# Idle bf16 products on TensorE in the drain and the first attention rounds of a decoder layer

## What is computed

```
x = LN(x + state_space(x))          # 16 states per feature, scan over the 64 tokens of a sequence,
                                    # layer norm inside, projection W_out
x = LN(x + gated_attention(x, ctx)) # 4 heads of 32, causal, weights q.k * exp(cumulated log gates - row max),
                                    # divided by max(|row sum|, exp(-row max)), norm per head
x = LN(x + moe(x))                  # router of 8 experts, top 2, silu(x w1) * (x w3) w2, hidden size 512
```

## Time and profile before

| | us |
|---|---|
| median of 3 runs | 702.19 (701.72, 702.19, 706.64) |
| profiled execution | 706.54 |
| its span, first to last instruction | 704.9 |
| TensorE busy | 544.6 (77%) |
| VectorE busy | 430.6 (61%) |
| GpSimd busy | 369.7 (52%) |
| ScalarE busy | 329.5 (47%) |
| mean granted TensorE clock | 0.863 |

### The profile page before, as it was taken

One profiled execution on the slowest core, in us unless ns is written; L12 is line 12 of the kernel. 1 busy time (PEld: TensorE's weight loads), 2 busy tenths in 40 slices (PEclk: granted clock), 3 DMA queues, 4 the chain that ended last, 5 costly groups with the idle time before them and its releaser, 6 DMA issues.

```text
span 704.9 us, 10813 instructions
## 1 busy us (share of the span) xinstructions
PE 544.6 (77%) x3387; PEld 386.7 (55%) x3387; DVE 430.6 (61%) x880; ACT 329.5 (47%) x732; POOL 369.7 (52%) x301
## 2 busy tenths in 40 slices
PE   2589999899889888686384889797878689989800
PEld 0234434445344447675263768686667568988800
DVE  1599999999999941676748376656352612211155
ACT  2475685876867553122132435444443323333327
POOL 1497979999789752216506163625253533322341
PEclk9999999999999995555555789998898899999955
DMA  4434535444454532732341735361616157788594
GB/s 148 148 101 148 175 122 166 146 170 167 137 179 146 191 74 52 133 62 62 77 113 42 193 120 158 136 232 36 203 63 216 59 177 243 241 292 270 170 244 117
DMA packets 83319, 104.51 MB, mean 148 GB/s; under 512 B 40784, under 2 KB 64592, under 8 KB 83136
## 3 DMA queue, kind: packets, MB, share of 16 engines
q1 hardware_dynamic: 74576, 90.99, 42.4%
q0 software_dynamic: 4320, 8.92, 3.7%
q10 hardware_dynamic: 4368, 3.93, 2.0%
HBM read 91.48 MB, written 12.34 MB: 147 GB/s over the span
## 4 chain that ended last, share of the span: by engine, by line
PE 25%; issue 24%; POOL 20%; DVE 10%; DMA 9%; ACT 3%; SPq 2%; another core or an unknown queue 1%; POOLq 0%; ACTq 0%; DVEq 0%
POOL hc L640 12%; PE pB L1063 7%; PE pq L1076 4%; DMA wslot<-in_expert_w 4%; PE py L818 4%; PE py L1063 2%; POOL y_dram L745 2%; PE pC L997 1%; ACT x_all L1457 1%; DMA y_dram<-dx,xin 1%; PE pa L979 1%; POOL xg_dram L736 1%; DMA x_all<-y_dram 1%; POOL bcs L604 1%
## 5 line engine op out<-in xcount | busy, mean ns | idle before, releaser
L640 POOL TENSOR_TENSOR hc<-h,Crep 128x1024 f32<-128x1024 f32 x64 | 149.7, 2356 | 14.6 <-DVE h L1507 13.2
L745 POOL DMA_INDIRECT y_dram<-dx,xin x71 | 68.9, 971 | 153.9 <-ACT dx L1378 144.8
L1063 PE MATMUL pB<-Crep,wslot 128*128 128x256 f32 (+1 forms) x556 | 118.9, 360 | 21.9 <-DMA wslot<-in_expert_w 10.7
L818 PE MATMUL py<-hc,ident 128*128 128x512 f32 x256 | 120.7, 598 | 8.1 <-POOL hc L640 8.1
L1063 PEld LDWEIGHTS pB<-Crep,wslot 128*128 128x128 f32 x556 | 90.8, 204 | 38.7 <-DMA wslot<-in_expert_w 14.0
L1498 DVE TENSOR_TENSOR u<-dx,pC 128x1024 f32<-128x1024 f32 x64 | 77.3, 1207 | 17.4 <-PE pC L807 17.3
L818 PEld LDWEIGHTS py<-hc,ident 128*128 128x128 f32 x256 | 46.8, 189 | 53.9 <-issue 37.4
L1789 DVE TENSOR_TENSOR Crep<-u,pB 128x512 f32<-128x512 f32 x35 | 24.0, 686 | 85.5 <-PE pB L1063 42.2
L1507 DVE TENSOR_TENSOR_SCAN h<-pB,u 128x1024 f32<-128x1024 f32 x32 | 73.1, 2285 | 1.0 <-ACT pB L1196 0.6
L1507 DVE TENSOR_TENSOR_SCAN h<-pa,u 128x1024 f32<-128x1024 f32 x32 | 73.1, 2284 | 0.0
L1789 DVE TENSOR_TENSOR u<-u,pB 128x512 f32<-128x512 f32 x36 | 24.8, 688 | 78.9 <-PE pB L1063 46.0
(11 more groups left out here) (225 smaller groups left out, 952.0 us busy)
## 6 DMA issues: line engine op xcount, KB each, us to landing
wslot<-in_expert_w SPq DMA_DIRECT2D x46, 768.0 KB
Crep<-c_dram SPq DMA_DIRECT2D x64, 512.0 KB, 3.8
h<-m_dram SPq DMA_DIRECT2D x16, 256.0 KB
xin<-xg_dram SPq DMA_DIRECT2D x25, 130.0 KB
cT_st<-in_ctx_T SPq DMA_DIRECT2D x8, 256.0 KB, 4.1
dx<-in_ctx_T SPq DMA_DIRECT2D x8, 256.0 KB, 4.0
delta<-in_ctx_tok SPq DMA_DIRECT2D x32, 64.0 KB
hc<-y_dram SPq DMA_DIRECT2D x8, 256.0 KB, 8.5
```

The source lines that it names most:

```text
L640: nc.gpsimd.tensor_tensor(hc[:, K % 4], h[:, K % 3], Crep[:, K % 4].rearrange("p a t -> p (a t)"), ALU.mult).then_inc(hc_done, 1)
L745: nc.gpsimd.indirect_dma_start(out=y2_dram, out_offset=bass.IndirectOffsetOnAxis(ap=xin[:, i % NX, a, D:D + 1].bitcast(i32), axis=0), in_= ...
L818: last = nc.tensor.matmul(py[:], ident[:], hc[:, K % 4, i * CH:(i + 1) * CH], start=False, stop=(K % STEPS == STEPS - 1 and i == 1))
L1063: last = nc.tensor.matmul(bank[:, o * a * P:(o + 1) * a * P], wslot[:, i % NW, stage * F + f * P:stage * F + (f + 1) * P], xgT[i % 2][:, 0 ...
```

## The change

A helper `fill(n)` issues `n` products of `sel[:, 0]` with `bcs[:, 0]` (96 rows, 128 by 512, bf16) into `py`. It waits for nothing and signals nobody; its result is overwritten unread. It is called at 9 places of the drain, at up to 8 places of the rounds 0 to 3, and in front of `turn_m(1)`. Nothing on the other engines is touched.

```
+            def fill(n):
+
+                for _ in range(n):
+                    nc.tensor.matmul(py[:], sel[:, 0], bcs[:, 0], start=True, stop=True)
+
             sum_state(STEPS * NCH - 2)
             sum_state(STEPS * NCH - 1)
             turn_m(0)
             center_y(NCH - 1)
+            fill(4)
             scores(0, 0)
             variance(NCH - 1)
+            fill(3)
             turn_x1(NCH - 2)
+            fill(3)
             scores(0, 1)
+            fill(3)
             project(NCH - 1)
+            fill(4)
             gate_products(NCH - 2)
+            fill(4)
             scores(0, 2)
+            fill(3)
             weighted_values(0, 0)
+            fill(3)
             scores(0, 3)
+            fill(3)
             weighted_values(0, 1)
...
+                if c <= 3:
+                    fill(4)
                 if back:
                     turn_x2(c - 1)
                 expert_units(first[0:1])
+                if c <= 3:
+                    fill(6)
                 if front:
                     scores(c + 1, 1)
+                if c <= 3:
+                    fill(4)
                 if back:
                     logits(c - 1)
                 expert_units(first[1:3])
+                if c <= 3:
+                    fill(8)
                 if front:
                     scores(c + 1, 2)
                 expert_units(first[3:])
+                if c <= 2:
+                    fill(6)
                 if front:
                     scores(c + 1, 3)
                     weighted_values(c + 1, 0)
+                if c <= 2:
+                    fill(4)
...
                 if front:
                     weighted_values(c + 1, 1)
                 expert_units(second[1:3])
+                if c <= 2:
+                    fill(8)
                 if back:
                     ranks(c - 1)
...
                 if c == 2:
+                    fill(16)
                     turn_m(1)
```

## The result

The changed kernel takes **732.24 us** (median of 5 runs, 726.75 to 734.83) against 702.19 before: ratio 1.0387, interval 1.0343 to 1.0431. It is slower by 4%. The ratios in this text are the recorded ones, for runs in the faster of two states, and not the quotients of the medians beside them (1.043 here).

What follows compares the result with a forecast made beforehand. It took the drain and rounds 0 to 3 as a chain passing between TensorE, at half clock, and VectorE. -0.3+0.5-4.5 = -4.3 from 706.54 gave 702.2; a middle value for the median was 700 us, range 690 to 716.

Steps and rivals of the forecast that it cites:

- Drain: From scores(0, 0) to the gate products: the clock holds, 8.57 us in place of 12.24, so -3.7 us.
- Round 0: Clock falls before scores(1, 0), fills cost 0.43 us, the drain's gain is given back; net of both stages -0.3 us.
- the twelve: Twelve fills in front of scores(1, 2) in round 0: 2.6 us if the clock is back, 5.1 if not.
- the wait for the heads: TensorE idle some 2.6 us before scores(1, 0), waiting for the context heads; the clock was taken to fall here.
- Rounds 1 and 2: 40 fills a round at 2.4 GHz, 8.6 us, in round 1 in waits for VectorE: +0.5 us, bounds 0 and +1.5.
- Round 3: Full clock from scores(4, 2) on, up to VectorE's product at 367.63: -4.5 us net, bounds -5.4 and +5.3.
- The rival that the products don't raise the clock: Everywhere: 96-row bf16 fills leave the clock low, 158 fills at 0.43 us: +40 us, so 740; chance 8%.
- The rival of the late clock: Fills before scores(1, 2) and scores(4, 2) run at half clock: +11 us, 713 to 717; chance 20%.
- The rival that the clock never falls: Clock up from the drain to round 3: -8.5 us, 698.0 for the profiled execution, 693.7 against the median; chance 20%.

Runs made afterwards that it cites:

- e15: Second trace of the changed kernel, nothing altered, a single execution on another chip: 708.18 us.
- e1: Changed kernel with only the 17 idle products of the drain up to the gate products, all others removed: 701.04 us, ratio 0.9979 to the kernel before.
- e7: Changed kernel without its 40 idle products in each of rounds 1 and 2: 712.54 us, ratio 1.0102 to the kernel before.
- e11: Changed kernel with every idle count from round 0 on halved, drain as in the change: 716.5 us, ratio 1.0216 to the kernel before.
- e13: As e3, f32 idle products, but over 96 of the 128 rows with the same streaming time: 737.49 us, ratio 1.0541 to the kernel before.
- e3: Changed kernel with idle products in f32 over 128 rows, same places and streaming time: 700.77 us, ratio 0.9997 to the kernel before.
- e16: Second trace of e3 (f32 idle products over 128 rows), nothing altered: 701.88 us.
- e6: Changed kernel with bf16 idle products over 128 rows, zeros in both operands: 714.63 us, ratio 1.0152 to the kernel before.
- e12: f32 128-row idle products only in the drain up to the gate products, before turn_m(1) and in round 3, three blocks longer: 703.68 us, ratio 1.0028 to before.

## Why the prediction was wrong, point by point

I said 700 us, 690 to 716, and 28% for slower by over 1%. It is 732.

- **Drain, -3.7.** Right in the profiled execution: the clock held at 1.00 to 275, and the gate products were done at 274.3 for 277.4, -3.2. That is partly luck: with the very same products in the drain, e15 kept the clock as well, but e1, e7 and e11 lost it at 266 to 268 in their traces. The step is a matter of the single execution, which I had not allowed for.
- **Round 0, gain given back, net -0.3.** Nearly right as a number, by another path: the clock was 0.50 from 276 to 289 and back for the twelve, and scores(1, 2) started at 293.47 for my 292.4; the net was +1.0. But the clock did not fall where I put it, in the wait for the heads. It fell at 275.6, 1.3 us behind `gate_products(6)`, with TensorE busy 3.38 of the 3.40 us from 272.3 to 275.7.
- **Rounds 1 and 2, +0.5 with bounds 0 and 1.5.** This is the step that failed: +11.8 and +8.8. I had costed the 40 products at 0.215 us because the forecast had the clock up when the round began and I saw no idle time in which it could fall. It fell at 302.9 at the end of round 0, after 12.50 us in which TensorE was busy all the time, and did not come back before 337. From there each idle product cost 0.43 us and more: 17.2 us of them in round 1, where TensorE had waited 4.7. Two things failed, then: I looked for falls only where TensorE is idle, and the forecast took it that idle products bring the clock back wherever they run. The second is the dear one, as e15 shows: the same fall, the clock back at 306, a round of 17.00 us. Why it came back there and not here stays open. The Trainium skill (TensorE: Matmul & The Clock Gate, HAM oscillation) puts the fall down to waits between bursts. The trace has a fall without a wait, and the measurement decides. The row that spoke against me was my own, 9.44 of 9.50 us at 0.50: I read it as saying that such work doesn't raise the clock and did not ask whether it could keep it.
- **Round 3, -4.5.** The clock was up from 365 to 374 and fell before scores(4, 3), so that the expert half-tile took 3.75 us as before: -0.6.
- **The rival that the products don't raise the clock,** 8%, +40 us. This is the one that came nearest: +30 by the medians. Its reason, 96 rows and not 128, is what e13 against e3 and e16 shows: 737, and 701 and 702. It is not the whole reason (e6, and the two faces of the changed kernel), and it is not absolute: ten of them after the transposes did raise the clock in round 0. I gave it 8% since I held the row count to be a detail. Its price was right in kind, 158 products of 0.43 us against 28 us of idle time, and that sum did not depend on anything unknown except the clock. (Its 740 is a slip: +40 makes 742 from the median and 747 from the profiled execution.)
- **The rival of the late clock,** 20%, had +3 for a cold round 1. By the prices of that same text a cold round is 11.2 us of real work and 17.2 of idle products in 16.3 us, +12. I never made that sum for one round, only for all four.
- **The rival that the clock never falls,** -8.5. e3 is nearly that: at 1.00 from 287 to 341, low for 3 us before and 7 us behind, and 699.74 us in its profiled execution for my 698.0. Over ten runs its ratio is 0.9997. So even with the clock kept, there was nothing to win that this measurement can tell.

Still open: why the clock falls behind the gate products and what decides whether it comes back, why the rows matter, whether the data do and how much (the runs of one kernel spread over 14 to 24 us there), whether the chip has a part in it, and why e12's gain shrinks among the expert tiles.

## What to carry to other kernels

Idle products that are to hold a clock are paid at the low clock whenever they fail, so cost each block at 1.2 GHz against the wait that covers it, round by round; here that was 17.2 us in round 1, where the wait was 16.30 - 11.63 = 4.7 us. Use all 128 rows and not zeros for them, and try the kind of product before the counts. And before holding the clock up in a stretch, ask whether a faster stretch reaches the end: here 8 us won early left 3.5 in one execution and nothing in the median. And trace a kernel twice before you explain its clock: two traces of this one differ by 11 us in a single round.

## What the runs showed of the hardware that I had not expected

The granted clock fell from 1.00 to 0.50 with TensorE busy 12.50 of 12.50 us before, and stayed at 0.50 through 34.00 us of unbroken work. In e16 it fell after 13.50 of 13.50 us busy (292.0 to 305.5), with idle products of 128 rows, and was back at 309. Idle f32 products over 96 rows gave 737.5 us and over 128 rows 700.8; bf16 over 128 rows 707.0 with ones and 714.6 with zeros; bf16 over 96 rows 732.2 with a selection matrix, 726.0 with ones and 716.6 with real data. But the last was measured on the chip on which the changed kernel's one execution took 708.2 us; its five others took 727 to 735.
